# Attention and expert layer on one core: the round of the attention phase in another order on every engine, and mean squares from split squares

## The reference, cut to what matters

```python
xn = layernorm(x)                               # 16 x 256 tokens of width 256
x  = x + attention(xn) + experts(xn)

# attention: 16 heads of 16, chunks of 64 tokens, no softmax
q = (q @ fq1.T + b1) * (q @ fq2.T + b2)         # k likewise
kv = exclusive cumulative sum over the chunks of k^T v
o  = q @ kv + tril(q k^T) @ v
o  = o * rsqrt(mean(o*o over a head) + 1e-5) * norm_w
return o @ wo.T

# experts: softmax of 8 router logits, top-p 0.9, each kept expert
out += (silu(x @ gate[e].T) * (x @ up[e].T)) @ down[e].T * w[:, e]
```

## Time and profile before

| | us |
|---|---|
| median of the runs (749.98 to 750.54) | 750.28 |
| the profiled execution | 747.49 |
| its span | 745.7 |
| TensorE busy in the span | 705.9 |
| VectorE | 484.6 |
| ScalarE | 411.9 |
| GpSimd | 363.3 |

### The profile page before, as it was taken

How to read it: one execution, slowest core, us unless ns; L and a number is a source line. 1 busy time by engine, 2 the same in 40 slices (tenths; PEclk the granted TensorE clock), 3 DMA queues, 4 the chain that set the end, 5 groups by cost and what they waited for, 6 DMA issues and landing times.

```text
span 745.7 us, 19643 instructions
## 1 busy us (share of the span) xinstructions
PE 705.9 (95%) x6664; PEld 658.0 (88%) x6665; DVE 484.6 (65%) x1079; ACT 411.9 (55%) x937; POOL 363.3 (49%) x385
## 2 busy tenths in 40 slices
PE   7899999999999975899999999999999999999992
PEld 6778778787877864899999999999999999999992
DVE  5878888787888793555756656655656656656551
ACT  4456667565666633555645556545655555546541
POOL 3023131313315333366666666666666666666663
PEclk9999999999999987899999999999999999999997
DMA  4413031111303233543634634533634534533332
GB/s 147 139 30 110 6 113 56 57 57 56 106 7 89 26 73 93 154 67 59 148 64 78 123 63 99 106 59 63 149 57 79 123 61 98 107 58 63 62 59 30
DMA packets 51860, 59.58 MB, mean 80 GB/s; under 512 B 9344, under 2 KB 48256, under 8 KB 51840
## 3 DMA queue, kind: packets, MB, share of 16 engines
q0 software_dynamic: 19776, 27.16, 22.8%
q1 hardware_dynamic: 32064, 32.16, 14.5%
HBM read 37.15 MB, written 22.15 MB: 80 GB/s over the span
## 4 chain that ended last, share of the span: by engine, by line
PE 67%; DMA 12%; issue 8%; POOL 5%; DVE 3%; POOLq 2%; ACT 2%; SPq 1%; DVEq 0%; ACTq 0%
PE A L1135 9%; PE A L1137 8%; PE A L1136 8%; DMA out<-ybuf,s_idx 7%; PE ring L1135 7%; PE ring L1136 6%; PE ring L1137 6%; PE ring L1208 4%; DMA xg<-gather_table,g_idx 4%; PE ring L1181 3%; POOL out L484 2%; POOL xg L468 2%; PE S L1137 2%; PE S L1136 2%; PE S L1135 2%
## 5 line engine op out<-in xcount | busy, mean ns | idle before, releaser
L484 POOL DMA_INDIRECT out<-ybuf,s_idx x98 | 160.9, 1641 | 62.4 <-POOL s_idx L480 46.6
L468 POOL DMA_INDIRECT xg<-gather_table,g_idx x100 | 100.4, 1004 | 89.5 <-issue 60.7
L1110 DVE TENSOR_TENSOR h_lo<-h,h_hi 128x256 fp32r<-128x256 f32 x196 | 83.7, 427 | 79.4 <-ACT h_hi L738 79.4
L738 ACT ACTIVATE h_hi<-h 128x256 fp32r<-128x256 f32 x196 | 81.9, 418 | 64.6 <-DVE h L1106 56.8
L1135 PE MATMUL ring<-w_hi,h_hi 128*128 128x256 f32 x392 | 114.2, 291 | 2.4 <-DVE h_lo L1110 2.4
L1135 PE MATMUL A<-gT_hi,w_hi 128*128 128x256 f32 x392 | 109.9, 280 | 1.6 <-DVE gT_lo L1079 1.6
L1136 PE MATMUL ring<-w_lo,h_hi 128*128 128x256 f32 x392 | 110.0, 281 | 0.0
L1137 PE MATMUL ring<-w_hi,h_lo 128*128 128x256 f32 x392 | 109.9, 280 | 0.0
L1136 PE MATMUL A<-gT_lo,w_hi 128*128 128x256 f32 x392 | 109.7, 280 | 0.0
L1137 PE MATMUL A<-gT_hi,w_lo 128*128 128x256 f32 x392 | 109.6, 280 | 0.0
L1135 PEld LDWEIGHTS ring<-w_hi,h_hi 128*128 128x128 f32 x392 | 74.4, 190 | 2.6 <-issue 2.6
(11 more groups left out here) (224 smaller groups left out, 2065.1 us busy)
## 6 DMA issues: line engine op xcount, KB each, us to landing
w_raw<-wffn SPq DMA_DIRECT2D x72, 192.0 KB, 2.9
xa<-x SPq DMA_DIRECT2D x8, 512.0 KB, 4.6
gather_table<-xna SPq DMA_DIRECT2D x8, 512.0 KB, 3.2
xr<-x SPq DMA_DIRECT2D x8, 512.0 KB, 4.1
out<-yout SPq DMA_DIRECT2D x8, 512.0 KB, 3.2
out<-ybuf,s_idx POOLq DMA_INDIRECT x104, 3.9
xg<-gather_table,g_idx POOLq DMA_INDIRECT x100
w_raw<-wqk_nat SPq DMA_DIRECT2D x1, 512.0 KB, 5.0
```

Source lines behind the costliest of these rows:

```text
L468: pool.indirect_dma_start(out=xg[:, sub, :], out_offset=None, in_=table, in_offset=bass.IndirectOffsetOnAxis(ap=g_idx[:, sub:sub + 1], axi ...
L484: pool.indirect_dma_start(out=out, out_offset=bass.IndirectOffsetOnAxis(ap=s_idx[:, sub:sub + 1], axis=0), in_=ybuf[:, sub, :], in_offset= ...
L738: a.activation(h_hi[:, ic, :], h[:, ic, :], ACT.Copy).then_inc(hhi_ok, 1)
L1110: v.tensor_tensor(h_lo[:, ic, :], h[:, ic, :], h_hi[:, ic, :].bitcast(F32), ALU.subtract).then_inc(hlo_ok, 1)
```

## The change

The lists of all engines are written in another order, and the mean square is taken in another way. ScalarE writes each square twice, rounded (`sq_hi`) and whole (`sq_raw`); GpSimd takes the difference (`sq_lo`), and TensorE makes two rounded products with a rounded `head_mean` in place of one full-float product. For the order some banks change: the fourth `values_logits` goes to `O[1]`, the two `keys_by_token` share `A[0]`, and the projections of q and the output move.

The diff, cut to its core:

```diff
-        sq = sb1("sq", [P, 2, BLK])
+        sq_hi = sb1("sq_hi", [P, 2, BLK], F32R)
+        sq_raw = sb1("sq_raw", [P, 2, BLK])
+        sq_lo = sb1("sq_lo", [P, 2, BLK], F32R)
...
-        q_banks = [(A[3], A[0]), (A[1], A[2])]
-        values_banks = [A[0], A[1], A[3], A[3]]
-        kt_banks = [A[0], A[1]]
-        wo_banks = [A[3], A[0]]
+        q_banks = [(A[3], A[0]), (A[1], A[3])]
+        values_banks = [A[0], A[1], A[3], O[1]]
+        kt_banks = [A[0], A[0]]
+        wo_banks = [A[1], A[3]]
...
+            def squares_low(s, half):
+
+                pool.wait_ge(sq_ok, 2 * s + half + 1)
+                g.tensor_tensor(sq_lo[:, half, :], sq_raw[:, half, :], sq_hi[:, half, :].bitcast(F32),
+                                ALU.subtract).then_inc(sqlo_ok, 1)
...
                 add_residual(s, 1)
+                squares_low(s + 1, 0)
                 tokens_low(s + 2)
+                squares_low(s + 1, 1)
...
-                a.activation(sq[:, half, :], O[half][:, :], ACT.Square).then_inc(sq_ok, 1)
+                a.activation(sq_hi[:, half, :], O[half][:, :], ACT.Square)
+                a.activation(sq_raw[:, half, :], O[half][:, :], ACT.Square).then_inc(sq_ok, 1)
...
                 logits_out(s, 1)
-                if not last:
-                    norm_refine(s + 1, chain)
                 softmax_head(s, chain)
...
+                queries(s, 1)
                 state(s, 0)
-                queries(s, 1)
                 if last:
                     one_hot(s - 1, 1)
+                else:
+                    norm_refine(s + 1, chain)
...
             def mean_squares(s, half):
-                pe.wait_ge(sq_ok, 2 * s + half + 1)
-                mm(ms_banks[half][:, :], head_mean[:, :], sq[:, half, :], start=True, stop=True).then_inc(ms_ps, 1)
+                pe.wait_ge(sqlo_ok, 2 * s + half + 1)
+                mm(ms_banks[half][:, :], head_mean[:, :], sq_hi[:, half, :], start=True, stop=False)
+                mm(ms_banks[half][:, :], head_mean[:, :], sq_lo[:, half, :], start=False, stop=True).then_inc(ms_ps, 1)
...
                 values_logits(s, 2)
                 pe.wait_ge(qk_ok, 4 * s + 2)
-                scores(s, 0, first)
                 values_logits(s, 1)
-                pe.wait_ge(lg_ok, 2 * s + 1)
+                if not first:
+                    pe.wait_ge(on_ok, 2 * s)
                 values_logits(s, 3)
+                scores(s, 0, first)
```

More of the change, by code:

```diff
@@ L624, in round_of @@
                 values_out(s, 1)
+                values_out(s, 3)
+                if not first:
+                    heads_hi(s - 1, 0)
+                    heads_hi(s - 1, 1)
+                keys_by_token(s, 0)
                 if not last:
                     token_rstd(s + 1)
[L627 to L630, removed]
                 queries2(s, 1)
@@ L633, in round_of @@
                 a.activation(ex[:, :, :], ls[:, :, :], ACT.Exp).then_inc(ex_ok, 1)
-                if not last:
-                    norm_apply(s + 1)
                 if last:
                     one_hot_tokens(s - 1)
+                else:
+                    norm_apply(s + 1)
+                queries_masked(s, 1)
                 keys2(s, 1)
-                queries_masked(s, 1)
-                if not first and not last:
-                    one_hot_tokens(s - 1)
-                squares(s, 0)
[L643 to L648, removed]
+                if not first:
+                    if not last:
+                        one_hot_tokens(s - 1)
+                    outputs_copy(s - 1, 0)
+                    keys_by_token(s, 1)
+                    outputs_copy(s - 1, 1)
+                else:
+                    keys_by_token(s, 1)
+                squares(s, 0)
                 if last:
@@ L651, in round_of @@
                     return
+                front(s + 1)
                 squares(s, 1)
@@ L932, in round_of @@
                     norm_stats(s + 1, chain)
-                if last:
+                logits_out(s, 0)
+                if not first:
                     one_hot(s - 1, 0)
-                logits_out(s, 0)
+                logits_out(s, 1)
                 masked_scores(s, 0)
                 masked_scores(s, 1)
-                logits_out(s, 1)
-                if not last:
-                    norm_refine(s + 1, chain)
                 softmax_head(s, chain)
-                if not first and not last:
-                    one_hot(s - 1, 0)
+                queries(s, 1)
                 state(s, 0)
-                queries(s, 1)
                 if last:
                     one_hot(s - 1, 1)
+                else:
+                    norm_refine(s + 1, chain)
                 masked_scores(s, 2)
                 masked_scores(s, 3)
+                keys(s, 1)
+                if not first and not last:
+                    one_hot(s - 1, 1)
                 softmax_tail(s, chain)
-                keys(s, 1)
                 choose(s, 0, chain)
@@ L970, in round_of @@
                 masked_scores(s, 5)
-                if first:
-                    choose(s, 2, chain, first)
+                choose(s, 2, chain, first)
+                state(s, 1)
                 masked_scores(s, 6)
-                state(s, 1)
                 masked_scores(s, 7)
                 if not first:
-                    one_hot(s - 1, 1)
+                    add_indices(s - 1)
                 slots(s, 0, chain)
@@ L981, in round_of @@
                 queries(s + 1, 0)
-                if not first:
-                    add_indices(s - 1)
                 if more:
                     norm_stats(s + 2, chain)
+                head_norm(s, 1, chain)
                 keys(s + 1, 0)
-                head_norm(s, 1, chain)
             chain = Chain(dve, dve_step, None)
@@ L1273, in round_of @@
                 pe.wait_ge(qk_ok, 4 * s + 2)
+                values_logits(s, 1)
+                if not first:
+                    pe.wait_ge(on_ok, 2 * s)
+                values_logits(s, 3)
                 scores(s, 0, first)
-                values_logits(s, 1)
                 pe.wait_ge(lg_ok, 2 * s + 1)
-                values_logits(s, 3)
                 keys_by_token(s, 0)
-                pe.wait_ge(s_ok, NPAIR * s + 1)
                 project(q_banks[1][1], 1, 1).then_inc(proj_ps, 1)
@@ L1287, in round_of @@
                 project(k_banks[1][0], 2, 1).then_inc(proj_ps, 1)
[L1288 to L1296, removed]
+                pe.wait_ge(qk_ok, 4 * s + 3)
                 if not first:
                     output_projection(s - 1, 0)
+                values(s, 0)
@@ L1299, in round_of @@
+                scores(s, 2)
+                if not first:
                     output_projection(s - 1, 1)
+                keys_by_token(s, 1)
+                if last:
+                    pe.wait_ge(y_ok, 2 * s + 1)
+                    slot_tokens(s - 1)
+                    pe.wait_ge(y_ok, 2 * s + 2)
+                    ranks(s, last_rank_bank)
+                values(s, 1)
+                state(s, 1)
+                scores(s, 3)
                 if last:
                     pe.wait_ge(rank_ok, s + 1)
-                keys_by_token(s, 1)
@@ L1303, in round_of @@
-                scores(s, 3)
-                if not last:
-                    pe.wait_ge(y_ok, 2 * s + 1)
+                    slot_tokens(s, last_idx_bank)
+                else:
+                    pe.wait_ge(y_ok, 2 * s + 2)
                     transposes(s + 1, 0)
-                    pe.wait_ge(y_ok, 2 * s + 2)
+                    pe.wait_ge(kv_ok, 2 * s + 2)
                     transposes(s + 1, 1)
[L1309 to L1312, removed]
+                    if not first:
+                        slot_tokens(s - 1)
```

40 lines of the change are left out of this document (21 added, 19 removed).

## The result

The changed kernel takes 760.25 us (median; 757.89 to 761.91) against 750.41 us for the kernel before on the same chip: a ratio of 1.0124 [1.0098, 1.0150], slower by 9.8 us. That is in the range, a quarter of a microsecond from its upper end. The profiled execution took 757.89 us, with a span of 756.1.

The account below looks back on a forecast made before the run. TensorE's own list was taken to bound rounds 1 to 6; 31.3 + 1.55 + 0.55 + 0.1 = 33.5 us against 32.67 gave +5.0, plus 0.5 in the last round: 755.8 us, range 744.5 to 760.5.

Parts of the forecast that it names:

- the means: On TensorE, two rounded products in place of each full-float mean square: 0.48 + 0.39 = 0.87 us saved a round.
- the longer runs: On TensorE, longer runs of like products in the new order: priced at +0.1 us, within bounds of -0.3 and +0.3.
- the clock: TensorE's granted clock was not expected to fall, since 2.2 us of waiting left it at 1.00 in round 0.
- TensorE's list: TensorE's own work in a round, without new waits: 32.06 - 0.87 + 0.1 = 31.3 us.
- Scores 3: TensorE waits for masks 4 and 5 from VectorE: 0.7 + 0.85 = 1.55 us a round.
- the path over normalization, `qz` and t2k: Chain through ScalarE and VectorE to masks 4 and 5: ready at 15.5 against TensorE's 14.8, a 0.7 us wait.
- k of the next round: TensorE waits ahead of `values_logits` 1, as GpSimd's difference holds the slot chain: 0.85 less 0.3, 0.55 us.
- Transposes for kv: `kv` may make TensorE's second transposes wait 0 to 0.4 us; 0.1 taken.
- No exclusion: Rival: comparisons and slots run through GpSimd's operations; rounds of 32.0 us, 746.8 us in all; chance 0.21.
- Only one of the two meets: Rival: only comparisons (751.9 us) or only slots (750.1 us) meet a GpSimd operation; chance 0.13.
- a meeting cost a whole GpSimd operation: Rival: each meeting costs 1.28 us and the transposes wait 0.4; rounds of 34.7 us, 762.8 us; chance 0.08.
- TensorE alone: Rival: normalization or k come earlier, so TensorE's work alone decides; rounds of 31.3 us, 742.6 us; chance 0.06.

Follow-up runs that it names:

- experiment 11: The changed kernel run again, unchanged: 757.60 us, ratio 1.0092 to the kernel before.
- experiment 8: Changed kernel with t2k ahead of the masked queries, GpSimd's first difference ahead of its second residual addition, and VectorE's statistics behind `on` and k: 742.85 us.
- experiment 7: Kernel before, old order, with the rounded means alone and GpSimd's differences of squares cut to 16 columns in place of 512: 747.80 us.
- experiment 4: Changed kernel with t2k of half 1 ahead of the masked queries on ScalarE: 749.63 us, ratio 0.9971 to the kernel before.
- experiment 5: Changed kernel with GpSimd's two residual additions a round cut to 16 columns in place of 512: 753.78 us.
- experiment 10: Changed kernel with t2k ahead of the masked queries and GpSimd's first difference ahead of its second residual addition, statistics not moved: 746.33 us.
- experiment 1: Kernel before in its old order, with only the mean squares taken in two rounded products: 751.29 us, ratio 0.9991 to the kernel before.
- experiment 6: Changed kernel with GpSimd's two differences of squares cut to 16 columns in place of 512: 758.00 us.
- experiment 2: The changed kernel's order with the full-float means of the kernel before: 758.64 us, ratio 1.0096 to the kernel before.
- experiment 3: Changed kernel with TensorE repeating a product of `state(s, 1)` six times more in rounds 1 to 6, inside its wait: 755.32 us.
- experiment 9: Kernel before, old order, with the rounded means and VectorE's statistics moved behind k and the second `on`: 755.60 us.

## Why the prediction was right, and where it was not

**The sign and the mechanism were right; the size was reached from two errors that nearly cancel (the means and the longer runs) and one that does not (the clock).** Rounds 1 to 6 were to lose 5.0 us together. The full-clock rounds lose 5.85 (five of 33.74 us and, from the rerun, a sixth of 33.19, against 196.04 us for the six before). The clock adds 4.6 us that the sum did not have (206.49 us measured for the six, less 201.89). With +0.6 us in round 0 (0 forecast), where the same path makes scores 2 wait 1.1 us, with +0.2 in the last round up to the start of its last product (250.40 to 291.12 us before, 261.16 to 302.05 after; 0.5 forecast), and with -0.3 ahead of the rounds and -0.6 behind, this makes the 10.4 us between the two profiled executions. Without the clock it would be 5.8 us, against 5.5 forecast. How much larger the whole loss is than that differs from one set of runs to the next: 9.8 us here, 7.2 in experiment 11.

**TensorE's list**, 31.3 us forecast: 31.33 in experiment 8, where nothing waits. But two terms of it were mis-sized. The means save 0.59 us (experiment 7), not 0.87. I read the first full-float mean as 0.94, all of it its own; in experiment 7 the two rounded products at that place take 0.61 us to the next start (0.54 in the changed kernel), not 0.46, and the product behind them takes 0.33 to the next start in place of 0.23, so part of the 0.94 is what any product pays there. The second mean came out as forecast (0.46). And the longer runs, which I priced at +0.1, come out at -0.14 (31.33 against 31.47), some of which may be the restart behind the `kv` wait that experiment 7 still has.

**Scores 3**, 1.55 us forecast, 1.71 waited: 0.73 of it the path over normalization, `qz` and t2k (0.7 forecast; experiments 4 and 5), the rest the comparison (0.85 forecast, 0.97 by rows, 1.39 - 0.42). That the 0.7 came out so exactly is in part luck: TensorE arrives 15.1 us behind the transposition (14.8 forecast), and the masks would be done 15.8 behind it without the meeting (15.5 forecast), both 0.3 late. That a meeting costs some 1 us fits the rule of the Trainium skill (SBUF — State Buffer, Who interferes with whom) that the later of the two waits to the end of the earlier: of GpSimd's addition 1.11 us were left when the comparison started (0.97 paid), of the difference 1.24 us when `lo_i` did (1.09 paid). The Trainium skill also says there that a reduction (`tensor_reduce`) never contends with GpSimd on trn2; `cum` at 0.42 us in experiment 4 agrees.

**k of the next round**, 0.55 us forecast. The wait in the row is 0.31 us, but what it costs is about 0.55: by so much the round that has no statistics ahead of k is shorter (33.19 against 33.73 in experiment 11), and by 0.56 experiment 8 is shorter than 10. That this is the number of the forecast is luck: the forecast was a wait, 0.85 less 0.3 to spare; the meeting took 1.09, and all but 0.31 of it was covered. The row of a wait shows less than its price. Products of this block start 0.12 us apart, but the starts around the wait are 155.68, 156.26 and 156.49, 0.57 us more for the two steps: the row counts idle time only from the end of the last product (0.28 us long), and the first product behind the wait takes 0.23 us to the next start. In full-clock rounds of the changed kernel 2.02 us of waiting make 33.74 - 31.33 = 2.41 us.

**Transposes for kv**, 0.1 forecast: no wait in the changed kernel. In experiment 4, where scores 3 no longer waits, it came up with 0.86 us.

**The step that failed** is "The clock I don't expect to fall." I took one wait of 2.2 us in round 0 that had left the clock at 1.00 as the rule for six waits of 1.7 us. That very wait, 2.17 us in round 0 of the old order, lowers the clock in experiment 1 (1.00 in the earlier trace rows):

```profile
23.14:55.10 31.96, 29.16 (x306) 23.67 (x305) 24.11 (x58) 16.73 (x35) 6.37 (x5) 0.95 0.23 65
```

The waits of 1.7 us, too, can go either way: three of six rounds in the first profile, two of six in the second, four of six in experiment 6, one of six in experiment 2, and none in the six rounds each of experiments 3 and 5, with waits of 0.37 and of 0.6 to 0.8 us. Each fall costs 1.5 to 1.6 us, nearly as much as the wait itself. Why the clock falls in one round and not in the next is not settled: the rounds have the same work and the same wait.

**The rivals.** "No exclusion" is out by experiments 5, 6 and 7. "Only one of the two meets" is out by the profile, in which both do. Nor did a meeting cost a whole GpSimd operation (0.97 and 1.09 us, not 1.28), and the transposes did not wait. "TensorE alone" describes not this kernel but the one of experiment 8: rounds of 31.33 us against that rival's 31.3.

## What to carry to other kernels

When an engine is to become denser, look for what the freed time runs into: here a wait removed uncovered a next one three times (experiments 4, 5 and 9; 0.2 to 0.9 us), and an operation moved by one place decided the sign. Ask of every GpSimd operation that is added or moved which VectorE operation stands beside it, and either move the GpSimd operation away (experiment 8's exchange leaves GpSimd idle while the last comparisons run, and none is held) or bring what bounds forward in the chain behind the meeting (k, which there no longer has the statistics ahead of it). And price a repeated wait of the bounding engine at more than its length: the restart behind it, and on TensorE perhaps the clock, count too.

## What the runs showed of the hardware

- TensorE's clock fell to half behind waits of 1.7 us in some rounds and not in others with the same work (long rounds 1, 2, 6 and then 1, 3 of one kernel), and behind a wait of 2.17 us in round 0 of experiment 1, but not behind the same wait in the kernel before. Filling the wait with useless products kept it at 1.00 in all six rounds (experiment 3).
- Very small operations are held like large ones: `tile_no`, four elements in each partition, took 1.24 us in the changed kernel's round 3 (0.16 before) beside GpSimd's `tokens_low`; a cast of 32 elements in each partition took 1.32 us in experiment 1 (0.18 before).
- The exclusion works the other way as well. In experiment 1 two `tokens_low` took 3.51 us together (3.54 in the kernel before): the second stands 2.27 us in its row, of which VectorE's `oh_lo`, started 0.15 us ahead of it, takes the first 1.1; in the changed kernel, where `oh_lo` stands elsewhere, they took 2.52.
